# A two-layer decoder on one core: pauses between indirect DMAs regrouped, routing of the second expert layer moved ahead, fewer expert blocks, and the front of self-attention rearranged

## What is computed

```python
x = _layernorm(x + _L0_attn_ref(...))    # causal self-attention, rotary, 16 heads, 4 key heads
x = _layernorm(x + _L0_xattn_ref(...))   # cross-attention
x = _layernorm(x + _L0_ffn_ref(...))     # 8 experts, top 2, width 1024, and one shared
x = _layernorm(x + _L1_attn_ref(...))    # RWKV recurrence
x = _layernorm(x + _L1_xattn_ref(...))   # cross-attention
x = _layernorm(x + _L1_ffn_ref(...))     # 16 experts, and two shared, below
```

```python
scores = jax.nn.sigmoid(x @ w_gate.T)
group_scores = jax.lax.top_k(sv, 2)[0].sum(-1)          # sv: scores in 4 groups of 4
top_groups = jax.lax.top_k(group_scores, TOPK_G)[1]     # 2 groups of the 4
_, idx = jax.lax.top_k(masked, TOPK)                    # 4 experts of the 8 left
w = w / (w.sum(-1, keepdims=True) + 1e-06)
g = jax.nn.silu(jnp.einsum('th,efh->tef', x, w1_e))     # F = 128
u = jnp.einsum('th,efh->tef', x, w3_e)
routed = jnp.einsum('tef,ehf,te->th', g * u, w2_e, combine)
shared = _swiglu(x, w1_s, w3_s, w2_s)
```

## Time and profile before

| | |
|---|---|
| median of three runs | 1544.47 us (1539.64 to 1547.03) |
| profiled execution | 1542.29 us, of which the span of the profile is 1540.5 us |
| granted clock of TensorE, mean | 0.89 |
| PE busy | 1243.2 us, 81% of the span |
| DVE busy | 703.4 us, 46% |
| ACT busy | 528.9 us, 34% |
| POOL busy | 438.5 us, 28% |

### The profile page before, as it was taken

How to read it: one execution, slowest core, us unless ns; L and a number is a source line. 1 busy time by engine, 2 the same in 40 slices (tenths; PEclk the granted TensorE clock), 3 DMA queues, 4 the chain that set the end, 5 groups by cost and what they waited for, 6 DMA issues and landing times. The chain is left out here.

```text
span 1540.5 us, 22586 instructions
## 1 busy us (share of the span) xinstructions
PE 1243.2 (81%) x6704; PEld 809.7 (53%) x6704; DVE 703.4 (46%) x1921; ACT 528.9 (34%) x999; POOL 438.5 (28%) x969
## 2 busy tenths in 40 slices
PE   5589898998788598999999999949878719985930
PEld 2234443443444396666776667835556417764720
DVE  2666666664455330222222222857746403423734
ACT  1157676777656321122222223223422002221210
POOL 4433233313323317000000001822322770044045
PEclk9579999999899779999999999969978859997965
DMA  3891000000000172111111101241000333454432
GB/s 123 279 364 60 1 0 1 0 1 1 1 1 1 48 299 95 38 34 33 35 34 33 35 25 35 86 166 72 1 0 25 111 114 120 144 161 126 143 118 89
DMA packets 74502, 117.61 MB, mean 76 GB/s; under 512 B 8160, under 2 KB 63456, under 8 KB 71456
## 3 DMA queue, kind: packets, MB, share of 16 engines
q1 hardware_dynamic: 59424, 85.94, 16.2%
q0 software_dynamic: 9216, 25.18, 5.2%
q10 hardware_dynamic: 5760, 5.25, 1.0%
HBM read 66.01 MB, written 50.33 MB: 76 GB/s over the span
## 5 line engine op out<-in xcount | busy, mean ns | idle before, releaser
L467 ACT ACTIVATE att_PT<-att_ST 128x1024 f32<-128x1024 f32 (+1 forms) x192 | 148.0, 809 | 67.3 <-PE att_ST L580 36.0
L1334 ACT ACTIVATE f_work<-f_bank,f_ub 128x128 f32<-128x128 f32 x320 | 87.1, 384 | 243.0 <-PE f_bank L1598 236.8
L499 DVE CUSTOM_DVE_ANT_0 att_junk<-att_RB,att_causal_q 128x128 f32<-128x128 f32 (+3 forms) x256 | 120.8, 487 | 62.0 <-PE att_RB L562 49.4
L1607 PE MATMUL f_bank<-wd_down,f_work 128*128 x640 | 144.8, 379 | 1.0 <-ACT f_work L1334 1.0
L1587 PE MATMUL f_bank<-wu_up,f_work 128*128 x320 | 144.1, 593 | 0.7 <-DVE f_work L1423 0.7
L562 PE MATMUL att_RB<-att_kT,att_qT 96*128 96x512 bf16 (+3 forms) x384 | 121.2, 355 | 25.0 <-DVE att_mx L499 9.1
L1298 POOL DMA_INDIRECT wu_up<-Yd,f_pos x32 | 31.9, 996 | 347.6 <-DMA Yd<-f_work 339.4
L1607 PEld LDWEIGHTS f_bank<-wd_down,f_work 128*128 128x128 f32 x640 | 118.5, 190 | 15.6 <-issue 1.2
L2555 PE MATMUL f_bank<-w_w,f_xT 128*128 x384 | 104.2, 418 | 20.1 <-DVE f_xT L2413 16.2
L1429 DVE COPY f_work<-f_bank 128x512 f32<-128x512 f32 x80 | 55.4, 692 | 123.0 <-PE f_bank L1587 123.0
L577 PE MATMUL att_ST<-att_qT,att_kT 128*128 128x512 bf16 (+3 forms) x384 | 101.8, 330 | 2.9 <-ACT att_PT L467 1.5
(11 more groups left out here) (421 smaller groups left out, 2264.7 us busy)
## 6 DMA issues: line engine op xcount, KB each, us to landing
Xd<-g_zero SPq DMA_DIRECT2D x1, 12288.0 KB, 53.8
f_xin<-Xd SPq DMA_DIRECT2D x48, 256.0 KB
Yd<-f_yo SPq DMA_DIRECT2D x48, 256.0 KB
wu_up<-up_w SPq DMA_DIRECT2D x9, 1024.0 KB, 17.7
wd_down<-down_w SPq DMA_DIRECT2D x9, 1024.0 KB, 16.2
Xd<-g_zero SPq DMA_DIRECT2D x1, 5120.0 KB, 17.3
f_work<-Xd SPq DMA_DIRECT2D x40, 128.0 KB, 2.0
Yd<-f_work ACTq DMA_DIRECT2D x40, 128.0 KB, 1.7
```

The lines of the kernel that those rows point to most:

```text
L467: act.activation(buf[:, :, 0:w], ST[:, 2 * (k % 2):2 * (k % 2) + 2, 0:w], ACT.Exp, scale=float(HD) ** -0.5).then_inc(exp_done, 1)
L499: dve.tensor_tensor_reduce(junk[:, k % RING, 0:w], RB[:, bank, 0:w], G.causal_q[:, 512 - w:512], 1.0, LOWEST, ALU.add, ALU.max, to).then_i ...
L1334: last = act.activation(hT[:, m, :], bank[:, TB_ + m // 4, (m % 4) * P:(m % 4 + 1) * P], ACT.Gelu, bias=ub[:, ds(e, 1), m])
L1607: mm = pe.matmul(bank[:, YB + u % 2, 0:D], hT[:, m, :], W.down[:, ds(e, 1), m, :].rearrange("p o c -> p (o c)"), start=(m == 0), stop=(m = ...
```

## The change

*Pauses.* `Chain.pause` replaces the linked memset. None is left in layer 0, in the first half's dispatch and in the second half's gather of layer 1. In the second half's dispatch and the first half's gather there is one of 128x768 elements after each DMA.

*Early routing.* The tiles and helpers of layer 1's router become a class `Route1`, opened before the recurrent stage. For the first half, new steps in the plan transpose the tokens (`tg`), score them (`lg`), choose in four parts (`c`), count (`ct`), place (`lc`) and send three of the 32 scatters (`sx`).

*Layer 1's order.* The stage transposes and scores only the second half, does half of the shared work before the loop, and the other half behind the loop. PE waits for both halves' positions before the loop. Parts of `choose` alternate with the shared products on DVE.

*Fewer blocks.* Layer 0 takes 39 blocks instead of 40; layer 1 takes 47 per half instead of 48, which makes 47 pairs instead of 48, of which pair 23 holds one block of each half.

*Front of self-attention.* `xTb` holds all tokens, the weights are loaded first and the tokens in three parts; POOL blanks the stacks before its constants; ACT makes the copies of stack 0.

```diff
+    def pause(self, tile):
+        self.link(self.eng.memset(tile, 0.0))
...
-    xTb = pj.sb("xTb", [P, KD, S])
+    xTb = pj.sb("xTb", [P, KD, T])
...
-            sp.dma_start(xTb[:, :, :], a["xT"][:, :, 0:S]).then_inc(x_in, 16)
             sp.dma_start(wqkv[:, :, :], a["Wqkv"]).then_inc(w_in, 16)
+            load_x(0)
             sp.dma_start(cos[:, :, :], a["cos"]).then_inc(c_in, 16)
             sp.dma_start(sin[:, :, :], a["sin"]).then_inc(c_in, 16)
+            load_x(1)
+            load_x(2)
             sp.dma_start(G.x_sb[:, :, :], a["x"]).then_inc(G.x_loaded, 16)
-            sp.wait_ge(qkv_ready, TB)
-            sp.dma_start(xTb[:, :, :], a["xT"][:, :, S:T]).then_inc(x_in, 16)
...
+            act.wait_ge(blanked, 1)
+            act.wait_ge(dve_chain, 2)
+            act.activation(ks(2), ks(0), ACT.Copy)
+            act.activation(ks(5), ks(0), ACT.Copy)
+            act.activation(qs(1), qs(0), ACT.Copy)
+            act.activation(qs(4), qs(0), ACT.Copy)
+            act.wait_ge(dve_chain, 6)
+            act.activation(ks(3), ks(1), ACT.Copy)
+            act.activation(qs(3), qs(2), ACT.Copy).then_inc(stack0_ready, 1)
...
-    ITEMS = 40
-    assert ITEMS >= T * K // P + E - 1
+    ITEMS = T * K // P + E - 1
...
                                             G.x_sb[:, t, :], None).then_inc(scattered, 16)
-                    ch.link(pool.memset(rest[:, :], 0.0))
...
+    put(("r", 3, 1), ("tg", 0, 0), ("tg", 0, 1), ("tg", 1, 0), ("tg", 1, 1), ("lg", 0, 0))
+    put(("rs", 3, 1), ("c", 0, 0))
+    put(("y", 3, 1), ("c", 0, 1))
+    put(("tx", 3, 1), ("c", 0, 2))
+    put(("s", 3, 0), ("c", 0, 3), ("ct", 0, 0))
+    put(("dn", 3, 0), ("lc", 0, 0), ("sx", 0, 2))
+    put(("o", 3, 0), ("sx", 2, 3))
...
-    ROUTED = 48
+    ROUTED = TH * P * K // P + E - 1
...
+    def scatter(self, pool, ch, G, Xd, n, lo, hi, rest):
+        pool.wait_ge(G.zeroed, 32)
+        pool.wait_ge(self.pos_ready, n + 1)
+        for m in range(lo, hi):
+            s, r = m // self.W.K, m % self.W.K
+            pool.indirect_dma_start(Xd[:, :], bass.IndirectOffsetOnAxis(self.pos[:, n, r, s:s + 1], 0),
+                                    G.x_sb[:, self.W.TH * n + s, :], None).then_inc(self.scattered[n], 16)
+            if rest is not None:
+                ch.pause(rest)
...
+            route.scatter(pool, ch, G, Xd, 0, SENT, SCATTERS, None)
+            route.scatter(pool, ch, G, Xd, 1, 0, SCATTERS, route.rest[:, :])
...
-                        ch.link(pool.memset(rest[:, :], 0.0))
+                        if n == 0:
+                            ch.pause(route.rest[:, :])
...
+            for m in range(2 * FIRST):
+                shared_product(m)
+                route.choose(dve, ch, 1, m)
             shared_sum(0)
+            dve.wait_ge(sums_ready, 1)
+            route.locate(dve, ch, 1, bank[:, SB_ + 1, 0:CE], bank[:, SB_ + 1, CE:2 * CE])
+            route.owners(dve, ch, 1)
+            shared_sum(1)
...
-            FROM = NH_ + 4
+            FROM = LAST[0] + 7
...
-            pe.wait_ge(sh_prod, 2 * NG)
-            pe.wait_ge(sh_added, 2 * NG)
+            pe.wait_ge(sh_prod, 2 * FIRST)
+            pe.wait_ge(sh_added, 2 * FIRST)
+            pe.wait_ge(pos_ready, 2)
```

More of the change, by code:

```diff
@@ L267, in _ @@
             pool.memset(v_sb[:, :, :, HD:HD + 1], 1.0).then_inc(v_blank, 1)
+            for p in range(2):
+                pool.memset(qst[p][:, :, :, MROW:P], 0.0)
+                pool.memset(kst[p][:, :, MROW + 3:P], 0.0)
+                pool.memset(kst[p][:, :, MROW:MROW + 3], 1.0)
+                last = pool.memset(mx[p][:, :, :, :], LOWEST)
+            last.then_inc(blanked, 1)
             G.constants(pool)
@@ L307, in _ @@
             pe.wait_ge(w_in, 16)
[L308 to L315, removed]
+            for t in range(NT):
+                if t * P in XCUT:
+                    pe.wait_ge(x_in[XCUT.index(t * P)], 16)
+                pe.wait_ge(v_read, t + 1)
+                for kk in range(KD):
+                    mm = pe.matmul(PQ[:, t % 2, 0:384], xTb[:, kk, t * P:(t + 1) * P], wqkv[:, kk, :],
+                                   start=(kk == 0), stop=(kk == KD - 1))
+                mm.then_inc(qkv_ready, 1)
     pj.close(G.spent)
-    qst = [sb(f"qst{p}", [P, TB, REP, P], BF16) for p in range(2)]
-    kst = [sb(f"kst{p}", [P, TB, P], BF16) for p in range(2)]
     qT = [sb(f"qT{p}", [P, REP, S], BF16) for p in range(2)]
@@ L367, in build @@
         ch.done(eng.tensor_tensor(qs(5), rest_q[p][:, :, :, :], qs(2), ALU.subtract))
-        ch.done(eng.tensor_tensor(ks(4), rest_k[p][:, :, :], ks(1), ALU.subtract))
+        last = eng.tensor_tensor(ks(4), rest_k[p][:, :, :], ks(1), ALU.subtract)
+        if not copies:
+            last.then_inc(ready, 1)
+            return
+        ch.done(last)
         eng.tensor_copy(qs(1), qs(0))
@@ L486, in _ @@
             dve.wait_ge(blanked, 1)
-            build(dve, ch, 0, 0, stack0_ready)
+            build(dve, ch, 0, 0, stack0_ready, copies=False)
+            ch.wait()
             def step(i, p, placed):
@@ L1168, in moe0_stage @@
     EARLY, GROUPS = NT // 4, NT // 2
+    STORES = [len(range(p, N, 2)) for p in range(2)]
     sc = Scope(nc, "f0")
@@ L1353, in _ @@
             for p in range(2):
-                act.wait_ge(stored[p], 16 * N // 2)
+                act.wait_ge(stored[p], 16 * STORES[p])
         @block.vector
@@ L2290, in _ @@
             result(N - 1)
+            for m in range(2 * FIRST, 2 * NG):
+                shared_silu(m)
         @block.vector
@@ L2577, in down @@
                 mm.then_inc(dn_ready, 1)
-            for i in range(NG):
+            for i in range(FIRST, NG):
                 turn_group(i)
-            pe.wait_ge(W.arrived, 16 * W.LOADS)
-            score(0)
-            score(1)
-            for kk in range(KD):
-                pe.wait_ge(copied[kk], NG)
+            score()
             shared_up(0)
-            count(0)
             shared_up(1)
```

467 lines of the change are left out of this document (268 added, 199 removed).

## The result

| | before | after |
|---|---|---|
| median | 1545.75 us (4 runs) | 1504.11 us (1499.11 to 1506.2, 4 runs) |
| ratio after to before | | 0.9733, 95% interval 0.9696 to 0.9771 |
| profiled execution, span | 1540.5 us | 1497.4 us |

A forecast was written before the change was run, and what follows sets the result against it. It took PE's matmuls as the bound, with PE standing mainly where indirect DMAs run densely and its results come late. Terms −14.5 −8 −2 +11 −59.5 −24 −6 sum to −103: 1439.5, plus 2.2, forecast 1442 us, range 1406 to 1494.

The forecast's parts named there:

- Layer 0's pauses: Dispatch and gather of layer 0: trains shorten without short pauses, late results even out; −2 us.
- bound of +15 on the dispatch: Layer 0's dispatch, put at 0: worst case +15 us, the whole train at one matmul per DMA.
- bound of +10 on the gather: Layer 0's gather, forecast at −2 us: worst case +10 us.
- Tail: Last up to the end: unpaused last gather beside shared work, some results late, 60 us instead of 66; −6 us.
- Recurrent stage: First half's routing moved into this stage adds PE, DVE and POOL work; +11 us, bounds +5 and +16.
- Start of the loop: Layer 1 loop starts 56 us after the stage's first matmul instead of 115.5; −59.5 us, bounds −74.5 and −40.
- Loop: Layer 1 loop: 47 pairs at 3.61 us plus 8 us lost in two long-paused trains; −24 us.
- Front: Front of self-attention: earlier loads, memsets off the path, copies on ACT; −14.5 us, bounds −7 and −16.
- One block less: Layer 0's routed blocks: one fewer at 7.98 us each, with no cover; −8 us.
- the one in which dense trains are worse than today's: Unpaused trains give late results from the start: loop start +19, layer 0 +15, tail +15, 1491 us; chance 0.18.
- The slower one: One indirect DMA lets through about one matmul whatever the spacing, so long trains hold the loop; 1584 us, chance 0.05.
- The fast one: Nothing comes late in unpaused trains, or too short to matter; loop start at 41 us, total 1412 us, chance 0.22.

The follow-up runs named there:

- h4_before_none: The kernel before without any pause, on a chip with late results; 1589.1 us, 1.025 of before.
- j0_after: The changed kernel, unedited, run again on a chip without late results; 1428.1 us, 0.972 of before.
- e1: The changed kernel with a 128x16 pause again in the four trains that have none; 1442.4 us, 0.982 of before.
- g1: The changed kernel with 128x16 pauses again in its four trains without one, repeated on another chip; 1441.3 us.
- i1: The changed kernel with 128x16 pauses again in its four trains without one, run in a later job; 1438.8 us.
- i3: The changed kernel with short pauses back in four trains, norm(0) four pairs later and the last shared sum ahead of the fifth tile; 1431.8 us.
- j1: Repeat of the changed kernel with short pauses back, norm(0) four pairs later and the last shared sum ahead of the fifth tile; 1431.2 us.
- i4: The changed kernel with pauses of 128x96 in both layer 0 trains and 128x128, 128x256, 128x384, 128x256 in layer 1's four; 1437.7 us.
- j4: Repeat of the changed kernel with a different pause per train, 128x96 in layer 0 and 128x128 to 128x384 in layer 1; 1439.9 us.
- e2: The changed kernel with 128x768 pauses after every layer 1 indirect DMA and two 128x96 memsets after each of layer 0; 1496.1 us, 1.018 of before.
- g2: The changed kernel with long pauses in all trains, repeated on another chip; 1491.1 us.
- j2: The changed kernel with long pauses in all trains, run in the last job; 1492.5 us.
- f1: The changed kernel, unedited, run again on a chip with late results; 1506.6 us, 0.963 of before.
- h0: The changed kernel, unedited, run again on a chip with late results; 1502.8 us, 0.970 of before.
- h3: The changed kernel without its long pauses, so without any, on a chip with late results; 1555.3 us, 1.003 of before.

## Why the prediction was wrong, step by step

The direction was right and the size was not: 1504 lies outside 1406 to 1494. Of the 60 us by which the spans differ from the sum, layer 0's pauses are 36, the tail 14, the recurrent stage 6.5 and the loop with its start 6; the other stretches took 2 less than forecast. By its own steps, against the stretches above:

- **Layer 0's pauses, forecast −2, measured +33.7: the step that failed.** It said that lateness comes at the 17th DMA, lasts the rest of the train, and that a shorter train therefore evens it out. The 17th DMA was about right for PE, which stands from 574, 21 us in; ACT's results are late from the 11th. Two things were wrong. A DMA without a pause takes a step of 1.27, not 1.0, so there was almost nothing to win from the train's length (39.6 us instead of 42.9). And how much gets through after that point depends strongly on whether the short pause stands there: 24 records in the last 21 us against 61. I priced the late part of both kernels alike, as "even"; the runs show some 12 us for one and 47 for the other. The gain of 2 without lateness was about right (4). h4_before_none shows that the missing pauses alone account for the loss. The bound of +15 on the dispatch held (+12.9), the bound of +10 on the gather did not (+20.8): The gather before shows one late handoff and PE busy 22.8 of 23 us, and I had read that as a train that late results hardly reach; the gather after has the same breaks of 1.8 us, only the short pauses are missing, and PE is busy 11.3 of 23.
- **Tail, forecast −6, measured +8.** The mechanism was named and priced too low: DVE stands 7.7 and 9.8 us for the two halves of a sum, where the last weighing before waited for a DMA, and DVE's order puts both ahead of two tiles that don't need them. In j0_after, without lateness, the tail is 62.7 us: so lateness costs 11.6 where 5 were allowed, and the other 7.7 are about what a step of 1.25 instead of 1.0 adds over 31 steps.
- **Recurrent stage, forecast +11, measured +17.5.** The 7.2 us of transposes and scores stand in the path as worked out. Taken too low: the clock. I credited 2.4 us for a fuller PE; instead `o` takes 3.75 us where it took 1.96, `y` 5.27 where it took 3.72 (granted clock 0.70 from 1146 to 1152, 1.00 from 1128.3 to 1132 before), and what follows runs at the lower level as before (0.51 from 1156 to 1175, 0.50 from 1140 to 1150 before). Taken too low as well: `locate` on DVE ahead of the last moments, and POOL's scatters, the third of which stands between the two halves of its last spread. The stretch is 50.5 to 52.4 us in every trace of the changed kernel and its variants, with lateness or without (timelines of PE before and after, and of POOL after):

```profile
1128.26 3.72 PE L2029 MATMUL rx_R<-rx_w,rx_rw 128*128 128x256 f32 x16
1146.37 5.27 PE L2088 MATMUL rx_R<-rx_w,rx_rw 128*128 128x256 f32 x16
```

```profile
1178.89 1.07 POOL L2240 DMA_INDIRECT Xd<-g_x,r_pos  x1 [0.46 <-issue]
1180.03 0.23 POOL L1837 TENSOR_SCALAR rx_rstd<-rx_mv 128x2 f32<-128x2 f32 x1
```

- **Start of the loop, −59.5 against −57.4 to the steady loop.** Right to 2 us, by luck in part: two errors cancel. Without lateness the first `up` comes at 44.9 us (j0_after), not 41, as the scatters take 1.27 us a step; and lateness then costs 13, not 15, with two late results of ACT's instead of three, one of them of 19.3 us.
- **Loop, −24 against −20.** The size was near by luck, its ground was not. I allowed 8 us for lateness in the long trains; there is none. What is lost is norm(0)'s wait for POOL, behind a train that the long pause has made 20 us longer. I had checked that the gathered rows arrive in time, and not what else is queued behind the gathers on POOL.
- **Front −14.5: first transposes at 43.5 instead of 57.0 (−13.5),** as forecast; 3.4 more come in self-attention afterwards. **One block less −8, measured −6.4.**

Of the rivals, the one in which dense trains are worse than today's is nearest: layer 0 lost twice its price and the tail its price, the loop's start nothing. But its ground, late from the start, did not come true: in the trace after the first waits on "remote" stand at the 13th to 17th DMA of their trains, and in layer 0 the first results that ACT gets late, by about 1 us, at the 8th and the 11th. Its sum was 1491. The slower one is refuted: beside the long trains the pairs take their 3.61 us. The fast one's condition, nothing late, held on the chips without lateness: 1428 there, where it says 1412, but as a gain of 40 us over a before of 1469, not of 130 over 1542; a trace from a chip with lateness could not show that.

What stays open: what the late results and DVE's lookups wait for, and why only some chips have it. That layer 0 of the changed kernel gets back some 30 us on a chip with lateness when the short pauses return follows from h4_before_none by reversal, but was not measured: all four jobs with such a kernel (e1, g1, i1 with i3, j1) ran on chips without. For the same reason neither the gaps between 0.4 and 1.0 us (i4, j4) nor long pauses in all trains (e2, g2, j2) were measured with lateness. Without lateness the kernel with no pause at all is the fastest measured, 1414 us (0.961 and 0.962 of before); with lateness the changed kernel as it stands is the fastest of the four measured. A version with short pauses in layer 0 and norm(0) four pairs later should take about 1504 less 28 to 34 less 11, some 1460 to 1465 us, on a chip with lateness: an estimate from the stretches, not a run.

## What to carry to other kernels

Before a pause between DMAs is removed or lengthened, its price is what it adds to the step between two DMAs, not to one instruction; and it buys or loses time on another engine, so each train must be weighed by what PE has to hand over beside it. A longer train also holds back whatever the same queue does behind it: look for the small vector work that others wait for. And a comparison of two kernels holds for the chip it was made on: here taking the long pauses out of the changed kernel costs 52 us on one chip and gains 14 on others.

## What the runs showed of the hardware

- Chips of one kind differ. The kernel before takes 1546, 1550 and 1565 us in three jobs and 1468 to 1472 in four others, on three chips, one of them met twice with the same outcome. Only the traces of the former have late results of PE beside trains of indirect DMAs.
- Where it exists and the DMAs stand 1.25 to 1.28 us apart, ACT begins to get results of PE late, by about 1 us at first, at the 8th to 11th DMA, and PE itself stands from the 14th to 18th until the train ends (layer 0's trains in after, f1, h0, h3, h4). At 1.38 ACT's result at the 12th is still on time (586.3 in before). At 1.98 us it is absent.
- The short pause, 0.1 us of step, decides how bad it is in layer 0: 24 matmul records in the last 21 us of the train without it, 61 with it. It is no cure: late in the longer train of 64 in before, 26 records pass in 42 us.
- It is not in PE's results alone: DVE's index lookups, 0.1 us apart otherwise, come up to 1.4 us apart late in such a train (after, h0, h3).
- An indirect DMA keeps POOL 0.95 to 0.97 us in the median, and without anything between the next follows 0.30 us later.
